# Attention, a quantised feed-forward and two layer norms on one core: a cast moved to GpSimd, a matmul moved forward, and the last batch's normalisations on VectorE

## The reference, cut to what matters

```python
# x: [16, 256, 128] float32; 16 heads of 8; weights float32
qkv = x @ attn_w.T + attn_b                     # q, k, v of each head
mask = arange(n)[:, None] <= arange(n)[None, :]
scores = einsum('bhki,bhqi->bhkq', k, q) / sqrt(8)
probs = softmax(where(mask, scores, -10000.0), axis=2)
combined = einsum('bhkq,bhkl->bhql', probs, v)
x = layernorm(x + combined_as_rows @ out_w.T + out_b)
lhs_scale = max(abs(x), axis=2) / 127           # one scale for a row
rhs_scale = max(abs(rhs), axis=0) / 127         # one for a column
ffn = int(round(x / lhs_scale)) @ int(round(rhs / rhs_scale))
x = layernorm(x + ffn * lhs_scale * rhs_scale)
```

## Time and profile before

| | |
|---|---|
| median of three runs | 243.31 us |
| the profiled execution | 243.84 us |
| its span, first to last instruction | 242.1 us |
| mean granted clock of TensorE | 0.924 |
| TensorE busy | 201.0 us (83%) |
| VectorE busy | 189.1 us (78%) |
| ScalarE busy | 159.8 us (66%) |
| GpSimd busy | 136.4 us (56%) |
| chain that ended last, by engine | PE 43%, DVE 28%, issue 11%, POOL 4% |

### The profile page before, as it was taken

The page is one execution under the profiler, slowest core; times in us unless marked ns, Lnnn a source line. Parts: engine busy times, 40 slices in busy tenths (PEclk is TensorE's granted clock), DMA queues, the critical chain, the costliest instruction groups (busy, mean ns, idle before and its releaser), DMA issues.

```text
span 242.1 us, 10958 instructions
## 1 busy us (share of the span) xinstructions
PE 201.0 (83%) x4335; PEld 132.3 (55%) x4335; DVE 189.1 (78%) x593; ACT 159.8 (66%) x349; POOL 136.4 (56%) x273
## 2 busy tenths in 40 slices
PE   6269869899899999989999999998998889998410
PEld 3147645556565656565656565656565556665200
DVE  2819745889888989898989898989899799835521
ACT  3820055667777878786878787878686778796330
POOL 7634053331718585858585858585854343565754
PEclk9855575999999999999999999999999999999975
DMA  5397476939382849585758583957565611010001
GB/s 150 132 245 152 149 145 190 227 114 231 83 230 59 203 132 206 162 178 155 162 160 175 163 179 118 219 157 164 157 139 160 105 28 26 26 47 27 11 12 43
DMA packets 48259, 32.83 MB, mean 136 GB/s; under 512 B 4688, under 2 KB 48208, under 8 KB 48208
## 3 DMA queue, kind: packets, MB, share of 16 engines
q1 hardware_dynamic: 48064, 31.93, 53.6%
q10 hardware_dynamic: 144, 0.20, 0.3%
HBM read 17.17 MB, written 14.68 MB: 132 GB/s over the span
## 4 chain that ended last, share of the span: by engine, by line
PE 43%; DVE 28%; issue 11%; POOL 4%; DMA 3%; ACT 2%; SPq 1%; POOLq 0%; DVEq 0%; ACTq 0%
PE pv_bank L946 11%; DVE query_max L675 9%; PE act_bank L965 6%; PE dve_bank L879 6%; PE dve_bank L1007 4%; DVE ends_max L675 3%; PE dve_bank L956 3%; DVE ffn L774 3%; PE act_bank L870 2%; PE dve_bank L889 2%; DVE heads L723 2%; PE act_bank L1017 2%; DVE stats L785 2%; DMA k_stat<-image 2%; DVE rden L716 2%
## 5 line engine op out<-in xcount | busy, mean ns | idle before, releaser
L494 ACT ACTIVATE probs<-act_bank 128x512 f32<-128x512 f32 x160 | 88.4, 595 | 31.6 <-PE act_bank L889 31.2
L675 DVE TENSOR_REDUCE query_max<-dve_bank 128x2 f32<-128x512 f32 (+1 forms) x96 | 62.9, 681 | 10.1 <-PE dve_bank L889 9.9
L879 PE MATMUL dve_bank<-k_stat,q_move 48*64 48x256 bf16 (+3 forms) x1024 | 63.7, 245 | 5.6 <-DVE query_max L675 2.7
L870 PE MATMUL act_bank<-q_move,k_stat 50*64 50x256 bf16 (+3 forms) x1024 | 60.2, 236 | 0.9 <-issue 0.9
L879 PEld LDWEIGHTS dve_bank<-k_stat,q_move 48*64 48x64 bf16 x1024 | 41.7, 112 | 24.7 <-DVE ends_max L675 6.7
L946 PE MATMUL pv_bank<-probs,v_stat 128*32 128x256 f32 (+3 forms) x1024 | 49.4, 307 | 0.7 <-issue 0.4
L675 DVE TENSOR_REDUCE ends_max<-dve_bank 128x8 f32<-128x512 f32 x64 | 42.9, 679 | 3.6 <-PE dve_bank L889 3.5
L889 PE MATMUL dve_bank<-causal_t,identb 64*64 64x256 bf16 (+1 forms) x320 | 43.5, 263 | 0.2 <-issue 0.2
L889 PE MATMUL act_bank<-causal,identb 64*64 64x256 bf16 (+1 forms) x320 | 41.6, 253 | 0.0
L870 PEld LDWEIGHTS act_bank<-q_move,k_stat 50*64 50x64 bf16 x1024 | 39.3, 108 | 2.1 <-issue 1.4
L446 POOL TENSOR_SCALAR rstd<-moments 128x2 f32<-128x2 f32 x32 | 7.5, 234 | 53.8 <-DVE moments L790 37.4
(11 more groups left out here) (91 smaller groups left out, 339.1 us busy)
## 6 DMA issues: line engine op xcount, KB each, us to landing
image<-qk_parts SPq DMA_DIRECT2D x32, 384.0 KB, 3.3
q_move<-image SPq DMA_DIRECT2D x32, 192.0 KB, 4.3
k_stat<-image SPq DMA_DIRECT2D x32, 192.0 KB, 4.3
xt_in<-xt_dram SPq DMA_DIRECT2D x16, 128.0 KB, 4.6
x_in<-x_dram SPq DMA_DIRECT2D x16, 128.0 KB, 2.2
out_dram<-o SPq DMA_DIRECT2D x16, 128.0 KB, 1.9
q_move<-shift SPq DMA_DIRECT2D x64, 4.0 KB
wqkv<-wqkv_dram ACTq DMA_DIRECT2D x1, 192.0 KB, 2.7
```

What stands on the lines that cost most here:

```text
L494: act.activation(probs[u][:, :], act_bank[at % ACT_BANKS][:, :], ACT.Exp, scale=SCALE).then_inc(act_emptied, 1)
L675: dve.tensor_reduce(top, keys, op=ALU.max, axis=AX.X).then_inc(dve_emptied, 1)
L870: pe.matmul(bank[64 * half:64 * half + 64, at:at + TOK - blk * KB], k_stat[slot][rows, head, blk * KB:(blk + 1) * KB], q_move[slot][rows, ...
L879: pe.matmul(bank[64 * half:64 * half + 64, at:at + keys], q_move[slot][rows, head, blk * KB:keys], k_stat[slot][rows, head, 0:keys], start ...
```

## The change

1. GpSimd makes the second part of batches 4 to 15, right behind its second copy of the first part; VectorE keeps that of batches 0 to 3.
2. TensorE's `feed_forward(b - 3)` moves from behind P·V to right behind the maxima's transpose, ahead of the projection of q and k and of the first group of P·V.
3. In the last batch (15) VectorE makes z from mean and factor, adds the residual and makes o; GpSimd makes only the first two of the four factor steps. From phase 16 on the three scale steps of a batch follow each other on VectorE, after the heads are normalised.

```diff
+POOL_SECOND = 3
@@ GpSimd, split
                     pool.tensor_copy(first_again[b % 2], first).then_inc(qk_split[1], 1)
+                    if b > POOL_SECOND:
+                        wait(pool, qk_split, b, 2)
+                        pool.tensor_copy(second, qk_rest[:, :, :]).then_inc(qk_split[1], 1)
@@ GpSimd, norm_factors
                 pool.tensor_tensor(t[:, 0, :], t[:, 0, :], minus_half[:, :], ALU.pow).then_inc(made[1], 1)
+                if b == NBATCH - 1:
+                    return
@@ GpSimd, add_residual and norm2; ScalarE, norm1
-                if not real(b):
+                if not real(b) or b == NBATCH - 1:
                     return
@@ VectorE
+            def last_norm1():
+                b = NBATCH - 1
+                wait(dve, rstd_made, b, 2)
+                for t in range(TILES):
+                    dve.tensor_scalar(z[b % RING][:, t, :], y[:, t, :], moments[0][:, t, 0:1], rstd[0][:, 0, t:t + 1],
+                                      ALU.subtract, ALU.mult).then_inc(z_made[1], 1)
+            def last_residual():
+                b = NBATCH - 1
+                wait_place(dve, dve_emptied, DVE_AT, ("ffn", b))
+                wait(dve, o_made, b - 1)
+                dve.tensor_tensor(r[:, :, :], ffn[:, :, :], z[b % RING][:, :, :], ALU.add).then_inc(r_made[1], 1)
+            def last_norm2():
+                b = NBATCH - 1
+                wait(dve, rstd2_made, b, 2)
+                dve.wait_ge(stored, 16 * b)
+                for t in range(TILES):
+                    dve.tensor_scalar(o[:, t, :], r[:, t, :], moments[1][:, t, 0:1], rstd[1][:, 0, t:t + 1],
+                                      ALU.subtract, ALU.mult).then_inc(o_made[1], 1)
@@ VectorE, phase
                     if u == 2:
                         first_sum(b - 2, 2)
+                        if b - 2 == NBATCH - 1:
+                            last_norm1()
                     if u == 6:
                         normalise(b - 1, 0)
-                        scales(b - 2, 0)
+                        if b < NBATCH:
+                            scales(b - 2, 0)
                         normalise(b - 1, 1)
+                        if b >= NBATCH:
+                            scales(b - 2, 0)
+                            scales(b - 2, 1)
+                            scales(b - 2, 2)
                     if u == 7:
+                        if b - 3 == NBATCH - 1:
+                            last_residual()
                         second_stats(b - 3, 0)
-                        scales(b - 2, 1)
+                        if b < NBATCH:
+                            scales(b - 2, 1)
                     if u == 8:
                         make_shift(b + 1, 1)
                         second_stats(b - 3, 1)
-                        scales(b - 2, 2)
-                        if b > -3:
+                        if b < NBATCH:
+                            scales(b - 2, 2)
+                        if -3 < b < 0:
                             second_part(b + 4)
             phases(phase)
+            last_norm2()
@@ TensorE, phase
                     if u == 3:
                         turn_maxima(b + 1, 0)
+                        feed_forward(b - 3)
                         if b >= 0:
                             project_qk(b + 4, 0)
                             project_qk(b + 4, 1)
                         pv(b, 0)
-                        feed_forward(b - 3)
```

## The result

The changed kernel takes 251.66 us (median of four runs: 248.42, 251.56, 251.76, 253.12); the kernel before took 243.28 us beside it. The ratio is 1.030 (95% interval 1.020 to 1.039), so it is slower, by about 7 to 8 us; a second comparison further down has 1.033 (1.028 to 1.039). The forecast was 249.2, with 251.0 as its upper end: the median lies 0.7 above that end, the ratio times 243.31, which is 250.5, lies inside. Ratios here leave disturbed runs out, the 253.12 one among them, so they can differ a little from the quotient of the medians given. The profiled execution is that of 253.12, span 251.4 against 242.1; a later profile of the same kernel (249.41) has the same periods and the same held copies.

The account below looks back on a forecast made before the run. A chain alternating between TensorE and VectorE each phase was taken to bound the kernel. Steady part 7.5, plus 0.3, less 1.9 for the tail gave +5.9 on 243.31: 249.2 us; eight-in-ten range 241.0 to 251.0, A's own 247.5 to 250.8.

Parts of the forecast that it names:

- case A: Main forecast, chance 0.56: VectorE's small copy falls behind GpSimd's subtraction in phases 3 to 11 and is held; 249.2 us.
- Part 2, the wait and the hold: Each steady phase: `feed_forward` waits 0.19 for its bank; VectorE's copy, behind GpSimd's subtraction, lasts until that ends, 1.04 later.
- Part 1: Phases 3 to 11: VectorE loses a 0.39 cast, gains 0.09 a phase, limited by TensorE's unit 9 of the max scores.
- The steady part: Phases 3 to 11: seven phases 0.95 longer, phases 6 and 11 (TensorE pauses) 0.42 longer; sum 7.5 us.
- Phases 13 to 15: Phase 13 nothing; `feed_forward` waits 0.1 in phase 14 and 0.2 in 15, together 0.3 us (bounds 0 and 0.5).
- Part 3: Last batch: VectorE makes z and o, 0.45 per pair of operations; the tail gains 1.9 us (ends 1.0 and 2.2).
- B: Rival, chance 0.14: the copy, although late, slips in ahead of GpSimd's subtraction in the seven phases, +0.04 each; 242.8 us.
- C: Rival, chance 0.10: `feed_forward` finds its bank free, the copy stays ahead of the subtraction, −0.15 in seven phases; 241.3 us.
- F: Rival, chance 0.04: batch 14's store or the scaling in between eats the drain's gain; with A 250.5 us.
- E: Rival, chance 0.06: additionally, the phase's first copy is held by one of `norm2`'s operations, 0.3 in nine phases; 252 us.
- D: Rival, chance 0.10: no copy is held in any phase, 6 and 11 included, nine times −0.15; 240.1 us.
- The signs: If right: copy near 1.1 us, period 12.9, new pause before unit 4's reduction, z within 0.5 us of the power.

Follow-up runs that it names:

- a second comparison: The changed kernel run again unedited, beside the kernel before on one chip: 250.35 us, ratio 1.033 (1.028 to 1.039).
- part 2 alone: The kernel before with only `feed_forward` moved ahead of the projection: 252.15 us, ratio 1.034 (1.030 to 1.038).
- changed kernel with `POOL_SECOND = 6`: The changed kernel, but GpSimd takes the second part only from batch 7 on: 251.01 us, ratio 1.034 (1.029 to 1.039).
- the one with more GpSimd work: The changed kernel with a 128x128-word clearing on GpSimd ahead of the residual add in phases 3 to 11: 243.16 us, ratio 0.994.
- between the two projections: The changed kernel with `feed_forward` between the q and k projections: copy kept, 241.69 us; copy as a reduction, 240.23; that with GpSimd's second part from batch 7, 239.08.
- part 1 alone: The kernel before with only GpSimd's second part of batches 4 to 15: 243.18 us, ratio 0.999 (0.995 to 1.002).
- the three kernels without part 1: The kernel before (243.28 us), it with only `feed_forward` moved (252.15), and it with only the small copy as a reduction (242.0).
- the changed kernel without the hold: The changed kernel with the small copy written as a maximum over one element (`tensor_reduce`): 242.96 us, ratio 0.988 (0.982 to 0.994).

## Why the prediction was nearly right, step by step

**The direction and the mechanism** were those forecast: case A. The sum said +5.9; measured are +8.4 (251.66 − 243.28) in the first comparison and +7.3 (250.35 − 243.04) in the second. Without the start, the profiled execution gives 7.51 + 0.57 − 1.47 = +6.6.

**Part 2, the wait and the hold:** `feed_forward`'s wait was taken as 0.19, measured are 0.21 ahead of L1068. Unit 4's reduction was to come 0.13 later, it came 0.09 later. The copy was to be 0.10 behind the subtraction and was 0.06 behind (0.05 in part 2 alone). The copy's end was to be 1.04 later; it was 1.06 later (0.10 by its start, 0.96 by its length).

**Part 1:** taken 0.09 a phase, measured 0.06 (11.97 to 11.91). The limit named, unit 9, is the right one: VectorE now idles 0.16 for it at 175.47. By the Trainium skill's rule that the prediction cites (Perfetto Trace Analysis, Optimizing Scalar/DVE Operations), that such a move might not help, it would have been nothing. The trace has the 0.06 in each of the undisturbed phases; in the total time it is too small to be seen.

**The steady part:** 7 × 0.95 + 2 × 0.42 = 7.5 forecast, 7.51 measured in phases 2 to 12. Six undisturbed phases (3 to 5 and 8 to 10) cost 0.99 to 1.00 each, phase 7 only 0.85, since it was itself 12.12 before. In phase 6 the mechanism was the one told: TensorE pauses (0.20), `feed_forward` does not wait for the bank, and the copy starts inside the subtraction. It starts 0.23 into it, not 0.45, and lasts 0.96; but since it ends with the subtraction either way, 12.52 became 12.97, +0.45 for 0.42. The changed kernel with `POOL_SECOND = 6` shows it with a longer pause (0.36): there the phase takes 12.97 with the pause and without it, so the hold swallows the pause. In phase 11 the pause did not occur; the full hold came instead, +0.49 by another path than the one told. Phase 12, put at nothing, gave back 0.21. That the sum agrees to 0.01 is luck: the hold cost some 0.25 more than forecast, and phase 12 took as much off.

**Phases 13 to 15:** +0.3 forecast for 14 and 15, measured 9.79 − 9.67 = 0.12 and 8.37 − 8.13 = 0.24, together 0.36. Phase 13, put at nothing, added 0.21; in part 2 alone it was 11.28, in the kernel before 12.07. TensorE pauses there in some profiles (0.62 at 202.65 in the changed kernel, 0.42 at 192.25 before) and not in others, so this 0.21 is not shown to be the change's.

**Part 3:** −1.9 forecast, −1.47 measured (within 0.05 of that in the repeated run). Two terms were mis-sized. The first is the pair of operations on VectorE, taken as 0.45: it takes 0.60, twice (z and o), so z stands 0.64 after the end of the power (L452, 240.66) instead of 0.49. The second is a step that failed. The prediction saw that batch 14's `ffn` scaling now queues behind z, and charged it to VectorE alone; it left the end of batch 14's `norm2` where it was, 5.22 us after the power. But `norm2` works on r, which waits for this scaling: r starts 1.24 us after the power (241.90 − 240.66) instead of 0.52, `norm2` ends at 5.46, and the last residual waits for it (246.22, 0.33 idle). From the end of the power to the end of the last residual it was 6.50 us and is 5.99, 0.51 earlier instead of about 0.8. The residual itself (0.43 against 0.42) was right. The last `ffn` came 0.47 earlier, not 0.92: besides z, the three scale steps, each now waiting for the one before, take 0.42, 0.24 and 0.17 with gaps between, instead of running under other work. That cost nothing in the end, since `norm2` was later still.

**The rivals.** B and C each described the steady phases of a kernel that was run. The copy slips in although `feed_forward` waits (B): that is the one with more GpSimd work, period 12.01, and B's price for a phase, +0.04, is what it shows (12.01 against 11.97). C's condition, a bank found free, holds between the two projections, and C's price of −0.15 is near the −0.17 there (11.97 to 11.80). So the alternatives were priced well, and which of them the unedited kernel fell to was decided by 0.06 us; the prediction could not know that side for certain and gave A 0.56. F did not come, though its scaling in between did take a part of the drain's gain. E's sign would have been holds of the phase's first copy: in phases 3 to 11 it stays at 0.17. D needed nine copies free; none was.

**The signs and the arithmetic.** The copies, the period and the new pause before unit 4 came as named. The sign that z would stand within 0.5 us of the power did not (0.64). GpSimd's second cast started 3.4 us ahead of the next factors, not 2 (171.95 to 175.35), because those moved back with the held copy. Two small slips stand in the prediction's numbers: slower was given 0.64, while A, E and F add up to 0.66; and waits of 0.75 to 1.15 in seven phases give 247.8 to 250.6, not 247.5 to 250.8.

**The median over the range.** The steady part's forecast stands, the drain gave 0.4 less and phases 13 to 15 cost 0.26 more; that would be 249.9. What is left, 1.8 us, is most likely the start, which the sum put at nothing; the median execution has no profile, so this is not shown. In the profiled executions phase 2's output projection starts anywhere from 56.7 to 61.1 us. The same kernel gave 56.72 and 60.56; the three kernels without part 1 lie between 57.6 and 58.4, but part 1 alone did not change the median. The prediction had one profile of before, at 57.87, and three runs within 0.7 us of each other, and took the start as fixed. Its range should have had some 2 us more on each side for that alone.

## What to carry to other kernels

When an edit shifts two engines against each other by a tenth of a microsecond, list the small VectorE copies near the start of long GpSimd operations. Each one that falls behind such a start lasts until that operation ends (1.13 us for 0.17 here), and on the path that costs more than the edit could gain. Whether casts and operations with two inputs are held in the same way no run here shows. A copy written as a `tensor_reduce` over one element was never held, behind the start or ahead of it (it made even the kernel before 0.4% faster), and one matmul group's place in the queue (between the two projections) can decide whether its bank is free. When an operation is put at the head of a queue for the last item, follow also what it pushes back on the item before, since they may share a buffer.

## What the runs showed of the hardware that was not expected

**How close the order is decided.** In every kernel that keeps the copy, those that started 0.05 to 0.55 us behind GpSimd's subtraction were held until its end; those that started 0.03 to 0.15 ahead never were. Between 0.03 ahead and 0.05 behind, no run shows which wins. The result is that more work on GpSimd made the kernel 8 us faster.

**The start.** After a burst of DMA at 44 to 48 us (share of the queues' time 1.03 in the profile of before), TensorE stands for 0 to 2.01 us with no reason that the profile shows ("issue"). In two of the thirteen profiles the granted clock fell at that time. TensorE of the first changed profile:

```profile
49.22 0.19 PE L912 MATMUL act_bank<-q_move,k_stat 50*64 50x64 bf16 x1 [1.45 <-issue]
...
50.67 2.08 PE L1007 MATMUL act_bank<-xt_in,wqkv 128*128 128x256 f32 x4
```

The same projection at the higher level takes 1.13 (before, and the changed kernel run again). The windows (length, then busy us of each engine, granted clock, DMA share, GB/s) of the first changed profile and of the repeated one:

```profile
48.00:52.00 4.00, 2.78 (x30) 1.99 (x30) 1.92 (x5) 1.29 (x4) 0.00 (x0) 0.68 0.21 76
```

```profile
48.00:52.00 4.00, 3.67 (x84) 2.42 (x83) 3.02 (x8) 2.79 (x6) 2.38 (x4) 1.00 0.25 77
```

The mean granted clock is 0.68 against 1.00: TensorE had stood 1.45 us, then the clock was at its lower level of 1.2 GHz for a while, and 0.95 us went to this projection alone. The other such profile is that of the changed kernel without the hold (pause 1.72); these two have the latest starts of phase 2, 60.56 and 61.05. With part 1 alone the pause was 1.75 and the projection took 1.13 all the same. The pause came in kernels with and without the change (0.88 in the profile of before, 1.20 with part 2 alone, none in the repeated run of the changed kernel, 2.01 with `POOL_SECOND = 6`). Why it comes stays open.
